# Two of four probability blocks through PV in three reduced passes, and PV two steps behind the scores

## The reference

```
sa, ca, ga, sb, cb, gb = six modulation vectors per batch, from silu(c) @ wmod
h = layernorm(x) * (1 + ca) + sa
q, k, v = h @ Wq + bq, h @ Wk + bk, h @ Wv + bv      (W = fp4 codes * block scales, 16 heads of 128)
out = softmax(q k^T / sqrt(128)) v                   (per batch and head, 512 x 512)
x = x + ga * (out @ Wo + bo)
h = layernorm(x) * (1 + cb) + sb
x = x + gb * (h @ W^T + top-2-of-8 gated LoRA of h)
```

## Time and profile before

| | us |
|---|---|
| median of 3 runs (lowest, highest) | 883.76 (882.42, 885.69) |
| the profiled execution | 881.12 |
| its span in the trace | 879.0 |
| TensorE matmul busy | 823.7 (94%) |
| VectorE busy | 617.1 (70%) |
| GpSimd, ScalarE busy | 404.1 (46%), 381.8 (43%) |

### The profile page before, as it was taken

How to read it: one execution, slowest core, us unless ns; L and a number is a source line. 1 busy time by engine, 2 the same in 40 slices (tenths; PEclk the granted TensorE clock), 3 DMA queues, 4 the chain that set the end, 5 groups by cost and what they waited for, 6 DMA issues and landing times.

```text
span 879.0 us, 13011 instructions
## 1 busy us (share of the span) xinstructions
PE 823.7 (94%) x3548; PEld 607.9 (69%) x3548; DVE 617.1 (70%) x1268; ACT 381.8 (43%) x852; POOL 404.1 (46%) x439
## 2 busy tenths in 40 slices
PE   3969899999999999999999999999999999998758
PEld 2746677777777777777777777777777777665556
DVE  3767676776777777777767777777777775767563
ACT  2543544444444445544444444544444443442321
POOL 4433355444544555445544554445545552433230
PEclk9999899999999999999999999999999999999889
DMA  6143334443344334443444335533443353333002
GB/s 199 50 111 109 80 83 106 130 123 93 90 131 134 94 89 113 138 118 88 112 132 115 89 89 140 140 88 89 130 133 98 90 154 94 76 84 78 19 1 96
DMA packets 73808, 90.61 MB, mean 103 GB/s; under 512 B 19571, under 2 KB 40501, under 8 KB 73781
## 3 DMA queue, kind: packets, MB, share of 16 engines
q1 hardware_dynamic: 55988, 74.02, 32.9%
q10 hardware_dynamic: 17792, 16.26, 6.2%
HBM read 21.01 MB, written 2.10 MB: 26 GB/s over the span
## 4 chain that ended last, share of the span: by engine, by line
PE 74%; SPq 8%; issue 6%; DVE 5%; POOL 3%; DMA 2%; ACT 2%; POOLq 0%; ACTq 0%; DVEq 0%
PE o_odd L938 12%; PE o_even L938 11%; PE score L878 8%; PE score L880 8%; PE score L879 8%; SPq L281 7%; PE qv L878 5%; PE qv L880 5%; PE qv L879 5%; PE ky L878 3%; PE ky L879 3%; PE ky L880 3%; POOL prob L364 2%; DVE neg_max L741 2%; DMA pT<-pB 1%
## 5 line engine op out<-in xcount | busy, mean ns | idle before, releaser
L364 POOL TENSOR_TENSOR prob<-prob,inv_sum 128x512 f32<-128x512 f32 x256 | 258.5, 1041 | 385.2 <-DVE inv_sum L746 384.9
L741 DVE TENSOR_REDUCE neg_max<-score 128x1 f32<-128x512 f32 x256 | 176.0, 691 | 195.7 <-PE score L880 195.4
L488 ACT ACTIVATE prob<-score,neg_max 128x512 f32<-128x512 f32 x256 | 175.6, 688 | 59.4 <-DVE neg_max L741 59.2
L752 DVE STREAM_TRANSPOSE pB<-prob 128x512 f32<-128x512 f32 x256 | 179.7, 703 | 8.8 <-POOL prob L364 1.0
L878 PE MATMUL score<-k_hi,q_hi 128*128 128x512 f32 x256 | 124.7, 487 | 6.6 <-ACT hT_hi L431 6.4
L938 PE MATMUL o_even<-pT,v 128*128 128x512 f32 x256 | 115.5, 593 | 1.9 <-DMA pT<-pB 1.9
L938 PE MATMUL o_odd<-pT,v 128*128 128x512 f32 x256 | 115.6, 594 | 1.6 <-DMA pT<-pB 1.6
L880 PE MATMUL score<-k_hi,q_lo 128*128 128x512 f32 x256 | 101.4, 396 | 0.0
L879 PE MATMUL score<-k_lo,q_hi 128*128 128x512 f32 x256 | 100.5, 393 | 0.0
L450 ACT ACTIVATE v<-qv 128x512 f32<-128x512 f32 x64 | 38.2, 597 | 134.9 <-PE qv L880 134.9
L701 DVE TENSOR_TENSOR yT<-score,yT 128x512 f32<-128x512 f32 x121 | 77.2, 676 | 3.9 <-PE score L880 3.9
(11 more groups left out here) (205 smaller groups left out, 1471.6 us busy)
## 6 DMA issues: line engine op xcount, KB each, us to landing
pT<-pB SPq DMA_DIRECT2D x1024, 64.0 KB, 2.0
out_dram<-x_nat SPq DMA_DIRECT2D x8, 256.0 KB, 2.1
stage<-in_L_attn_wv_codes_dram ACTq DMA_DIRECT2D x7, 256.0 KB
stage<-in_L_attn_wv_scales_dram ACTq DMA_DIRECT2D x14, 128.0 KB
stage<-in_L_attn_wq_codes_dram ACTq DMA_DIRECT2D x7, 256.0 KB
stage<-in_L_attn_wq_scales_dram ACTq DMA_DIRECT2D x14, 128.0 KB
stage<-in_L_attn_wk_codes_dram ACTq DMA_DIRECT2D x7, 256.0 KB
stage<-in_L_attn_wk_scales_dram ACTq DMA_DIRECT2D x14, 128.0 KB
```

Source lines behind the costliest of these rows:

```text
L364: pool.tensor_tensor(prob[:, i], prob[:, i], inv_sum[:, i:i + 1].to_broadcast([P, S]), ALU.mult).then_inc(prob_ok, 1)
L488: act.activation(prob[:, i], score_ps[i][:, :], ACT.Exp, bias=neg_max[:, i:i + 1], accum_out=row_sum[:, i:i + 1]).then_inc(exp_ok, 1)
L741: dve.tensor_reduce(neg_max[:, i:i + 1], score_ps[i][:, :], AX.X, ALU.max, negate=True).then_inc(max_ok, 1)
L752: dve.transpose(pB[:, s % 2, :, i].rearrange("p g k q -> p k g q"), prob[:, i].rearrange("p (k g q) -> p k g q", k=QT, g=G)).then_inc(pB_o ...
```

## The change

- `SPLIT = 2`: of the four blocks of PV the first two go through `three`, six matmuls of fp32r; the other two stay float32. All four add into one bank, `o`; the second PV bank becomes a bank of the output projection, `y`.
- For this ScalarE makes `pT_hi` (`prob_high`, two operations a step) and `v_hi` (in even steps), VectorE makes `pT_lo` (`prob_low`, two operations a step, ahead of the step's maxima), GpSimd makes `v_lo` (`v_low`, in even steps).
- PV runs two steps behind the scores: in step n TensorE does PV of n-2 right after the scores of n and ahead of the projections, instead of PV of n-1 at the step's end.
- On VectorE o_low goes behind the second turn and q_low behind the third. On ScalarE v's copy goes to the start of the next step and o_high behind the exponentials. GpSimd's work on weights is dealt out anew over the steps, and the high part of the v weights goes to ScalarE.
- After step 63 two PVs are left instead of one: PV(62) ahead of `ffn_input(0)`, and PV(63) ahead of `rows_of_y(2)`, behind it before.

```diff
+SPLIT = 2
+v_hi = sb("v_hi", [P, 2, SPLIT, PW], f32r)
+v_lo = sb("v_lo", [P, 2, SPLIT, PW], f32r)
+pT_hi = sb("pT_hi", [P, SPLIT, S], f32r)
+pT_lo = sb("pT_lo", [P, SPLIT, S], f32r)
...
-o_ps = [bank("o_even"), bank("o_odd")]
-y_ps = score_ps[2:4]
+o_ps = [bank("o"), bank("y")]
+y_ps = [o_ps[1], score_ps[3]]
...
+    def v_low(count, par):
+        pool.wait_ge(v_hi_ok, count)
+        pool.wait_ge(v_ok, 2 * count - 1)
+        pool.tensor_tensor(v_lo[:, par], v[:, par, 0:SPLIT], v_hi[:, par].bitcast(f32), ALU.subtract).then_inc(v_lo_ok, 1)
+
+    v_low(1, 0)
...
-            if s < 2:
-                if s == 0:
-                    product("o", p)
+            if s % 2 == 0 and not (first and s == 0):
+                v_low(B * p + s // 2 + 1, batch_of(s) % 2)
+            if s == 0:
+                product("o", p)
+            elif s < 3:
                 if not first:
-                    pool.wait_ge(y_mm, DC * (n - 1))
-                parts("o", p, s)
+                    pool.wait_ge(y_mm, DC * (n - 2))
+                parts("o", p, s - 1)
             elif not last:
-                if s < 5:
-                    product("vqk"[s - 2], p + 1)
-                elif s == 6:
-                    pool.wait_ge(v_mm, n + 2)
-                    parts("v", p + 1, 0)
-                else:
-                    pool.wait_ge(k_mm, n + 2 if s == 5 else n + 1)
-                    parts("q", p + 1, s // 6)
-                    parts("k", p + 1, s // 6)
+                if s == 3:
+                    product("v", p + 1)
+                    product("q", p + 1)
+                elif s == 4:
+                    product("k", p + 1)
+                elif s > 5:
+                    if s == 7:
+                        pool.wait_ge(w_hi_ok["v"], p + 2)
+                        pool.tensor_tensor(w_lo["v"][:, :, :], w32["v"][:, :, :], w_hi["v"][:, :, :].bitcast(f32),
+                                           ALU.subtract).then_inc(w_ok["v"], 1)
+                    pool.wait_ge(k_mm, n + 1)
+                    parts("q", p + 1, s - 6)
+                    parts("k", p + 1, s - 6)
             elif s in (4, 6):
                 gate((s - 4) // 2)
...
+        ps = qv_ps[:, :].rearrange("p (t f) -> p t f", t=2)
+        if half == 0:
+            act.activation(v_hi[:, par], ps, ACT.Copy).then_inc(v_hi_ok, 1)
+        act.activation(v[:, par, 2 * half:2 * half + 2, :], ps, ACT.Copy).then_inc(v_ok, 1)
...
+    def prob_high(par, have):
+        act.wait_ge(p_land[par], have)
+        for kt in range(SPLIT):
+            act.activation(split(pT_hi, kt), turned(par, kt), ACT.Copy).then_inc(p_hi_ok, 1)
...
-            if not early:
-                o_high(n - 1, s % 2)
-            if s == 1:
-                if not early:
-                    act.wait_ge(o_hi_ok, n - 1)
-                act.activation(bias_now[:, 2], bias[:, 2, bass.ds(2 * p, 2)], ACT.Copy).then_inc(bias_ok, 1)
-                act.wait_ge(bias_ok, 2 * p + 2)
+            if not start:
+                v_out(n + 1, batch_of(s) % 2, s % 2)
+            if s == SPP - 1 and not last:
+                act.wait_ge(w_prod["v"], p + 2)
+                act.activation(w_hi["v"][:, :, :], w32["v"][:, :, :], ACT.Copy).then_inc(w_hi_ok["v"], 1)
...
-                    act.activation(gb_row[:, 2 * i:2 * i + 2], (ky_ps, qv_ps)[i][:, :].rearrange("p (b d) -> p b d", b=2),
+                    act.activation(gb_row[:, 2 * i:2 * i + 2], (ky_ps, o_ps[0])[i][:, :].rearrange("p (b d) -> p b d", b=2),
                                    ACT.Copy).then_inc(gbb_ok, 1)
+            if not early:
+                o_high(n - 1, s % 2)
+            if s == 1:
+                if not early:
+                    act.wait_ge(o_hi_ok, n - 1)
+                act.activation(bias_now[:, 2], bias[:, 2, bass.ds(2 * p, 2)], ACT.Copy).then_inc(bias_ok, 1)
+                act.wait_ge(bias_ok, 2 * p + 2)
...
-            if not end:
-                v_out(n + 2, batch_of(s + 1) % 2, (s + 1) % 2)
+            if not start:
+                prob_high((s - 1) % 2, landed(p, s - 1))
...
     ffn_input_out(1)
+    prob_high(1, landed(PAIRS - 1, SPP - 1))
     o_high(N, 1)
...
+    def prob_low(n, par):
+        for kt in range(SPLIT):
+            dve.wait_ge(p_hi_ok, SPLIT * n + kt + 1)
+            dve.tensor_tensor(split(pT_lo, kt), turned(par, kt), split(pT_hi, kt).bitcast(f32),
+                               ALU.subtract).then_inc(p_lo_ok, 1)
...
                 dve.wait_ge(ld_x[new], 16)
+            if not early:
+                prob_low(n - 2, s % 2)
             maximum(0)
             maximum(1)
...
             inverse(1)
             if new:
                 row_statistics(new, 1)
-            if not early:
-                o_low(n - 1, s % 2, head_slice(p, s - 2))
             inverse(2)
...
...
                 variances(new)
             inverse(3)
             turn(1)
-            if not end:
-                q_low(n + 2, head_slice(p, s + 1))
+            if not early:
+                o_low(n - 1, head_slice(p, s - 2))
             turn(2)
             if new:
                 normalise(new)
+            if not end:
+                q_low(n + 2, head_slice(p, s + 1))
             turn(3)
             if not end:
...
     N = SPP * PAIRS
+    prob_low(N - 2, 0)
     attended(1)
-    o_low(N - 1, 0, slice(FEAT // P - 2, FEAT // P - 1))
+    o_low(N - 1, slice(FEAT // P - 2, FEAT // P - 1))
     ffn_rows(0)
     for c in range(DC):
         y_add(DC * (N - 2) + c + 1, B - 1, c, False, y_ps[c])
     ffn_rows(1)
+    prob_low(N - 1, 1)
...
-    o_low(N, 1, slice(FEAT // P - 1, FEAT // P))
+    o_low(N, slice(FEAT // P - 1, FEAT // P))
...
-    def weighted(vpar, j, par, have):
-
+    def weighted(n, vpar, j, par, have):
+
+        for kt in range(SPLIT):
+            pe.wait_ge(p_lo_ok, SPLIT * n + kt + 1)
+            cut = (slice(None), vpar, kt, slice(j * HD, (j + 1) * HD))
+            three(o_ps[0][:, :], (v_hi[cut], v_lo[cut]), (pT_hi[:, kt], pT_lo[:, kt]), kt == 0, False)
         pe.wait_ge(p_land[par], have)
-        for kt in range(QT):
-            ins = pe.matmul(o_ps[par][:, :], v[:, vpar, kt, j * HD:(j + 1) * HD], turned(par, kt),
-                            start=(kt == 0), stop=(kt == QT - 1))
+        for kt in range(SPLIT, QT):
+            ins = pe.matmul(o_ps[0][:, :], v[:, vpar, kt, j * HD:(j + 1) * HD], turned(par, kt),
+                            start=False, stop=(kt == QT - 1))
         ins.then_inc(o_mm, 1)
...
+                if i == 3 and not (first and s < 3):
+                    pe.wait_ge(y_ok, DC * (n - 2))
...
+            if not early:
+                pe.wait_ge(v_ok, n - s % 2)
+                pe.wait_ge(v_lo_ok, B * p + (s - 2) // 2 + 1)
+                if first and s == 2:
+                    pe.wait_ge(h_hi, DC * 2)
+                if not (first and s < 3):
+                    pe.wait_ge(o_ok, n - 2)
+                if end:
+                    pe.wait_ge(gbb_ok, 2)
+                weighted(n - 2, batch_of(s - 2) % 2, s % 2, s % 2, landed(p, s - 2))
             if end:
-                pe.wait_ge(gbb_ok, 2)
+                pe.wait_ge(v_ok, n + 1)
                 rows_of_y(0)
...
                 for c in range(DC):
-                    pe.wait_ge(exp_ok, QT * n + c + 3)
+                    if c:
+                        pe.wait_ge(exp_ok, QT * (n + 1))
                     out_project(c, s % 2, y_ps[c])
...
                 project_v(batch_of(nxt), nxt % 2).then_inc(v_mm, 1)
-            if not start:
-                pe.wait_ge(v_ok, n + s % 2)
-                if first and s == 1:
-                    pe.wait_ge(h_hi, DC * 2)
-                if not (first and s < 3):
-                    pe.wait_ge(o_ok, n - 2)
-                weighted(batch_of(s - 1) % 2, (s - 1) % 2, (s - 1) % 2, landed(p, s - 1))
...
+    pe.wait_ge(o_ok, N - 2)
+    weighted(N - 2, (B - 1) % 2, 0, 0, landed(PAIRS - 1, SPP - 2))
     ffn_input(0)
     pe.wait_ge(o_ok, N - 1)
     for c in range(DC):
-        pe.wait_ge(y_ok, DC * (N - 2) + c - 1)
+        pe.wait_ge(y_ok, DC * (N - 3) + c + 1)
         out_project(c, 0, y_ps[c])
     lora_rows(0)
     ffn_input(1)
+    weighted(N - 1, (B - 1) % 2, 1, 1, landed(PAIRS - 1, SPP - 1))
     pe.wait_ge(y_ok, DC * (N - 1))
     rows_of_y(2)
-    weighted((B - 1) % 2, 1, 1, landed(PAIRS - 1, SPP - 1))
     lora_rows(1)
     ffn_input(2)
     pe.wait_ge(o_ok, N)
-    out_project(0, 1, o_ps[0])
+    out_project(0, 1, y_ps[0])
     pe.wait_ge(x1_ok, 5)
-    out_project(1, 1, y_ps[0])
+    out_project(1, 1, score_ps[2])
```

21 lines of the change are left out of this document (9 added, 12 removed).

## The result

The changed kernel takes 873.52 us (median of 7 runs, 872.83 to 878.03) against 883.76 (7 runs, 878.91 to 885.69): a ratio of 0.9918, 95% interval 0.9898 to 0.9938. The ratio is an estimate from all runs of both kernels; the two medians alone lie 10.2 us, or 1.2%, apart. By the ratio the kernel is faster by 0.8%, where the prediction had 1.7% (14.8 us). The profiled execution took 872.83 us, the shortest of its seven, with a span of 871.0, 8.0 us less than the span before; the prediction's sum had 13.8. So the direction and the range held, and the gain was about half of what was forecast.

The account below looks back on a forecast made before the run. TensorE was taken to set the loop's time. Loop -19.5, first pair -1.4, last pair -5.4 and end +12.5 gave -13.8 from the profiled 881.12, so 867.3, or 870.0 from the median; predicted 869 us, range 860 to 879.

Parts of the forecast that it names:

- The loop: The 48 loop steps: TensorE's step falls from 11.71 to 11.36 and late landings are mostly recovered; -19.5 us.
- late landings: In the loop, probability blocks landing too late for PV; 3.2 us lost before, 0.5 left for them after the change.
- First pair: Steps before the loop: no gain until step 4, then four steps at 0.36 each; -1.4 us, bounds +2 and -6.
- Last pair: Steps 56 to 63: shorter steps 2.5, k projection's waits gone 2.4, late landing 0.5; -5.4 us, bounds -2.5 and -6.5.
- The end: Work from step 63 on: three places where the new work stands in series; +12.5 us, from +12.1 to +13.7.
- Place 3: From ffn_input(1) to rows_of_y(2): copies, prob_high, prob_low and PV(63) now come between; +5.6 to +7.2 us.
- -0.9 given back: In the end: o_low(63) no longer waits behind attended(2), which returns 0.9 us.
- what follows 832.40 stays as it is: The end's last stretch, behind 832.40 us in the profile before, was taken as unchanged.
- The end costs little: Rival, 10%: in the end the clock stays high and attended(0) isn't held; +6.5 instead of +12.5, 863 us.
- Half the loop's gain into new waits: Rival, 15%: landing, ScalarE's loads and v_hi meet in steps 1 to 4, exceeding VectorE's spare; +10, 879 us.
- VectorE becomes the bound: Rival, 9%: in the loop slower subtractions make VectorE set the step, more likely 12.0 us; about 912 us total.
- The passes don't run at 0.227: Rival, 6%: PV's passes on TensorE take longer than 0.227 us, so nothing is gained; 883 to 890 us.

Follow-up runs that it names:

- e1: Changed kernel with only the new order: all four probability blocks in plain float32, no high and low pieces; 888.72 us, ratio 1.0068 to the kernel before.
- e2: Changed kernel with PV of steps 62 and 63 in plain float32, without prob_high and prob_low for these two; 870.06 us, ratio 0.9861.
- e4: Changed kernel with the whole end put in another order on the engines, nothing left out; 861.38 us, ratio 0.9761.
- e10: Changed kernel with unread products of 512 columns filling TensorE's idle time behind the loop; 871.52 us, ratio 0.9891.
- e6_two_more: Changed kernel with two more unread subtractions behind prob_low in every step on VectorE; 890.10 us, ratio 1.0101.
- e7_passes_lag_one: Kernel before, PV still one step behind the scores, with only the three passes for two probability blocks and their pieces added; 988.89 us, ratio 1.1158.
- e9: e4 with three of the four probability blocks in three passes, instead of two; 858.45 us, ratio 0.9726.
- e13: e9 with the third subtraction of a step put behind VectorE's second maximum instead of ahead of the first; 861.01 us, ratio 0.9769.
- e14: e13 with TensorE's gaps in the end filled with unread products; 859.03 us, ratio 0.9742.
- e17: e14 with GpSimd making wv_lo of the next pair ahead of v_lo in step 7 of a pair; 853.67 us, ratio 0.9688.
- e8_columns_between: Changed kernel with the modulation's 32 four-column products in four groups of 8 between the score blocks of step 59; 874.94 us, ratio 0.9919.

## Why the forecast was right in sign and too large

- **The loop, -19.5 against -18.6.** The mechanism was right: two subtractions in 1.28, the maxima behind them, no waiting TensorE. The sizes were slightly off, and in both directions: two blocks gave 0.32 a step and not 0.36, a step of 11.39 and not 11.36, which is 1.4 us; the 0.5 left for late landings wasn't needed, since e1 recovers all 3.35.
- **First pair, -1.4 against -0.5.** Within its bounds, and within the 1 to 3 us by which this part differs between kernels with the same code there. The way was not as drawn, so that the nearness is luck: the first maximum of step 4 came 3.0 us later than before (90.77 against 87.75), that of step 5 only 0.55 later, and that of step 8 0.45 earlier.
- **Last pair, -5.4 against -4.9.** TensorE's four waits in the k projection (0.4 to 0.7 us) are gone, as forecast. The stretch with the columns gained a half clock behind them in the changed kernel (at 725 us) that the kernel before doesn't have. With the columns between the scores the part is -6.5. In the traces of e2 to e4, whose code there is that of after, it was -3.3: there the clock fell already among the columns and stayed low until 728 to 730 us. The forecast had no term for it.
- **The end, +12.5 against +16.0. This is the step that failed.** It makes 3.5 of the 5.8 us by which the sum of -13.8 missed the -8.0. The chain to ffn_input(0) was right to 0.1 us (+7.3, forecast 7.4); at ffn_input(1) it is +6.6. Place 3 cost +7.3, just over its bounds, where the sum had counted 6.0; 1.6 of it was the half clock in PV(63) (e10), which the forecast had priced at 1.5 and taken only in part. The "-0.9 given back" came to nothing: 0.7 us were given back, and lost in z rows that ran beside GpSimd. And "what follows 832.40 stays as it is" put at nothing what measured 2.2 us: a half clock behind a gap that had grown to 4.99. With 0.2 less behind it this is 6.6 + 7.3 + 0 + 2.2 - 0.2 = 15.9. The prediction knew the price of that clock (the same eight transposes at 1.97 and 1.10) and charged it at PV(61), PV(62) and PV(63), but not at the gap in front of ffn_input(2), which the order it had worked out made longer: before, TensorE waited 1.57 us there.
- **The rivals.** "The end costs little" was wrong for this kernel and right for e4_end_reordered, whose end costs +2.3, less than its 6.5. "Half the loop's gain into new waits" and "VectorE becomes the bound" didn't come; by e6_two_more VectorE becomes the bound only with two more subtractions in a step. "The passes don't run at 0.227" was wrong: in the loop the six passes of a PV take 1.36 us (403.98 to 405.34), 0.227 each.
- **Median and profile.** The profiled spans differ by 8.0, the medians by 10.2 us. With runs of one kernel 5 to 7 us apart, the 2 us between are within the measurement.

## What to carry to other kernels

A lag that makes room in a loop is paid where the loop ends, and there the order of each engine has to be written again: the order that is right for a step put three waits in series that cost 14 of the loop's 19 us, and a new order gave them back. When a forecast puts or lengthens a gap in front of TensorE, it should count the half clock behind this gap as a term with its own bounds, down to the last one: the work that took 6.42 us took 8.60. And two halves of a change can each lose alone, 0.7% and 12% here, and gain together.

## What was not expected of the hardware

- The clock can fall in the middle of a loop: in e7_passes_lag_one it did behind waits of 1.80 us (0.87 granted over 13 us), and not behind those of 0.76 (1.00). The length of the wait alone doesn't decide: behind 2.04 us rows_of_y(3) ran at the full clock in the kernel after (1.07) and at half in e10_gaps_filled (1.89).
- TensorE can lose the clock without having waited, behind products of four columns: 32 of them in 3.63 us in the kernel after, with 0.80 granted over the 8.5 us around them, and likewise in e2 to e4, e9, e10, e13, e14 and e17. The kernel before, e1_order_only and e6_two_more have the same 32 with the clock at full behind them, as e8_columns_between has behind four groups of 8. So they don't always bring it, and what decides stays open. The kernel before:

```profile
736.00:745.00 9.00, 9.00 (x57) 6.96 (x56) 2.93 (x5) 1.28 (x2) 0.39 (x1) 1.00 0.33 81
```

- VectorE and GpSimd slow each other when both read SBUF twice: 0.63 becomes 1.02 a subtraction, 0.62 becomes 1.06 a multiplication. It took a fuller VectorE, in e6_two_more, to make this cost a step anything. The z rows, with one wide input, are slower beside GpSimd too: 1.37, 1.94 or 2.65 us for the same four.
